# One core, conv attention and tanh attention: the planner of a hand-ordered kernel gets new spans, a longer hand-over between engines, and another rank for the score products

## The reference, cut to what matters

```python
# layer 0: conv attention (per image, HW = 4096)
e1, e2, asm = prelu(w1 @ gn(x)), prelu(w2 @ gn(x)), prelu(wa @ gn(x))
x = x + softmax(e1^T e2, axis=2) @ asm
# layer 1: additive (tanh) attention over earlier tokens
t = tokens(x);  n = layernorm(t)
f, g = n @ W1[:128], n @ W1[128:]              # 16 units each
scores[i, j] = sum_a w2[a] * tanh(f[i, a] + g[j, a] + b1[a]) + b2
t = t + (exp(scores) * (j < i)) @ n / sum_j(...)
# layer 1: 64 experts, each takes its 8 strongest tokens, two dense layers with gelu
```

## Time and profile before

| | |
|---|---|
| median of 3 runs | 5871.09 us (5862.58 to 5873.55) |
| the profiled execution, its own time | 5872.08 us |
| its span | 5869.9 us |
| PE busy | 5078.5 us |
| ACT busy | 4930.1 us |
| DVE busy | 2663.9 us |
| POOL busy | 2001.5 us |
| mean granted TensorE clock | 0.96 |

### The profile page before, as it was taken

How to read it: one execution, slowest core, us unless ns; L and a number is a source line. 1 busy time by engine, 2 the same in 40 slices (tenths; PEclk the granted TensorE clock), 3 DMA queues, 4 the chain that set the end, 5 groups by cost and what they waited for, 6 DMA issues and landing times. The chain is left out here.

```text
span 5869.9 us, 71555 instructions
## 1 busy us (share of the span) xinstructions
PE 5078.5 (87%) x28567; PEld 1726.0 (29%) x28567; DVE 2663.9 (45%) x3558; ACT 4930.1 (84%) x4186; POOL 2001.5 (34%) x1643
## 2 busy tenths in 40 slices
PE   6999988889999978899999987889999987666657
PEld 2333332223333323222333333222333332111113
DVE  8853474433454466443453466443354454000132
ACT  0139969999989969999959969999978969999970
POOL 1474431125454431113464441112555451111110
PEclk8999999999999999999999999999999999888977
DMA  0000000000000010000000010000000010000028
GB/s 29 12 18 8 8 29 1 1 8 6 13 19 10 9 40 8 1 1 8 19 19 4 12 44 8 1 1 8 10 22 10 12 38 17 1 1 1 6 101 283
DMA packets 39418, 123.99 MB, mean 21 GB/s; under 512 B 4464, under 2 KB 5424, under 8 KB 31984
## 3 DMA queue, kind: packets, MB, share of 16 engines
q1 hardware_dynamic: 38272, 119.03, 6.1%
q10 hardware_dynamic: 816, 0.39, 0.0%
HBM read 89.85 MB, written 29.56 MB: 20 GB/s over the span
## 5 line engine op out<-in xcount | busy, mean ns | idle before, releaser
L890 ACT ACTIVATE tanh_slots<-query_part,key_part 128x2048 f32<-128x2048 f32 (+41 forms) x3072 | 4151.5, 1449 | 149.0 <-DVE key_part L1293 101.5
L946 PE MATMUL ps<-tanh_slots,packed 128*32 128x512 f32 (+2 forms) x18432 | 2080.7, 588 | 457.4 <-ACT tanh_slots L890 449.5
L846 POOL TENSOR_TENSOR context_and_exp_sums<-context_and_exp_sums,exp_scores 128x512 f32<-128x512 f32 (+3 forms) x544 | 632.8, 1185 | 2043.4 <-ACT exp_scores L902 1615.5
L946 PEld LDWEIGHTS ps<-tanh_slots,packed 128*32 128x32 f32 x18432 | 541.2, 113 | 1931.1 <-ACT tanh_slots L890 1094.3
L1369 DVE TENSOR_TENSOR _tokens_second_and_probs<-ps,e_and_minus_max 128x1024 f32<-128x1024 f32 x512 | 624.5, 1220 | 1059.5 <-PE ps L981 534.4
L859 POOL TENSOR_TENSOR conv_prob_sums<-conv_prob_sums,_tokens_second_and_probs 128x512 f32<-128x512 f32 x480 | 613.6, 1278 | 1151.6 <-ACT _tokens_second_and_probs L907 1146.5
L981 PE MATMUL ps<-_tokens_second_and_probs,asm_tokens 128*128 128x512 f32 x2048 | 995.6, 612 | 6.8 <-ACT _tokens_second_and_probs L907 6.8
L907 ACT ACTIVATE _tokens_second_and_probs<-_tokens_second_and_probs 128x1024 f32<-128x1024 f32 x512 | 549.2, 1073 | 454.2 <-DVE _tokens_second_and_probs L1369 454.1
L1345 DVE TENSOR_REDUCE row_max_parts<-ps 128x1 f32<-128x1024 f32 x512 | 608.4, 1220 | 452.6 <-PE ps L1060 440.6
L1205 DVE TENSOR_TENSOR context_and_exp_sums<-context_and_exp_sums,ps 128x512 f32<-128x512 f32 (+3 forms) x544 | 344.7, 638 | 717.6 <-PE ps L957 713.3
L861 POOL TENSOR_TENSOR conv_prob_sums<-conv_prob_sums,_tokens_second_and_probs 128x512 f32<-128x512 f32 x480 | 617.6, 1287 | 37.7
(11 more groups left out here) (156 smaller groups left out, 2062.4 us busy)
## 6 DMA issues: line engine op xcount, KB each, us to landing
y_scratch<-residual_chunks SPq DMA_DIRECT2D x64, 256.0 KB, 2.0
tanh_slots<-in_wg SPq DMA_DIRECT2D x16, 1024.0 KB, 10.5
residual_chunks<-y_scratch SPq DMA_DIRECT2D x63, 256.0 KB, 2.7
residual_chunks<-in_x SPq DMA_DIRECT2D x32, 256.0 KB, 2.8
e_and_minus_max<-p_scratch SPq DMA_DIRECT2D x32, 256.0 KB, 3.3
query_part<-in_x SPq DMA_DIRECT2D x4, 1024.0 KB, 6.0
normed_tokens_first<-in_x SPq DMA_DIRECT2D x4, 1024.0 KB, 8.5
p_scratch<-e_twice SPq DMA_DIRECT2D x4, 1024.0 KB, 6.8
```

What stands on the lines that cost most here:

```text
L846: pool.tensor_tensor(dst, dst, src, ALU.add).then_inc(s_ds, 1)
L890: nc.scalar.activation(S[:, 4 * (R % 2) + k, q:SUP], F[:, SUP * blk.s + q:SUP * blk.s + SUP], ACT.Tanh, bias=keypart(blk.b, kg, kg + 1)).t ...
L946: last = mm(PS[32 * k:32 * k + 32, t, off:CHUNK], w2k[:, g, :], S[:, 4 * (R % 2) + k, CHUNK * t + off:CHUNK * t + CHUNK], start=(g == 0), ...
```

## The change

No instruction is added, removed or altered. `HOP` goes from 0.08 to 0.5 us, twelve planned spans change by up to 0.1 us, and the rank of `QK` goes from 4 to 2.5, which is behind `TR` and ahead of `C`, `F2a`, the `L` and gate work and `M`.

```diff
-    HOP = 0.08
+    HOP = 0.5
@@ T
-                prior_t = put("ACT", "T", (R, k), 0.1 + 0.833e-3 * (SUP - x.start(k, g)), behind, 4)
+                prior_t = put("ACT", "T", (R, k), 0.19 + 0.833e-3 * (SUP - x.start(k, g)), behind, 4)
@@ TR
-                prior_tr = put("PE", "TR", (R, t), 0.03 + 0.86 * w, behind, 2)
+                prior_tr = put("PE", "TR", (R, t), 0.02 + 0.89 * w, behind, 2)
@@ E, K, C
-        prior_e = put("ACT", "E", (n, t), 0.12 + 0.45 * w, behind, 1)
+        prior_e = put("ACT", "E", (n, t), 0.19 + 0.43 * w, behind, 1)
-            done.append(put("DVE", "K", (n, t), 0.35, [prior_e], 0))
-        put("PE", "C", (n, t), 0.05 + 0.86 * w, done, 3)
+            done.append(put("DVE", "K", (n, t), 0.3, [prior_e], 0))
+        put("PE", "C", (n, t), 0.07 + 0.88 * w, done, 3)
@@ conv pairs
-                put("PE", "QK", (P,), 1.1, behind, 4)
+                put("PE", "QK", (P,), 1.1, behind, 2.5)
-                put("DVE", "SM", (P,), 1.25, behind, 1)
-                put("ACT", "EX", (P,), 1.0, [("DVE", "SM", P), ("ACT", "EX", P - 1) if P else None], 2)
+                put("DVE", "SM", (P,), 1.2, behind, 1)
+                put("ACT", "EX", (P,), 1.05, [("DVE", "SM", P), ("ACT", "EX", P - 1) if P else None], 2)
-                put("POOL", "PS", (P,), 2.6 if p else 1.3, behind, 3)
+                put("POOL", "PS", (P,), 2.7 if p else 1.3, behind, 3)
@@ row maxima
-            put("PE", "M", (b, m), 0.9, behind + [("DVE", "M", b, m - 2) if m >= 2 else None], 4)
-            put("DVE", "M", (b, m), 1.25, [("PE", "M", b, m), ("DVE", "M", b, m - 1) if m else None], 4)
+            put("PE", "M", (b, m), 1.0, behind + [("DVE", "M", b, m - 2) if m >= 2 else None], 4)
+            put("DVE", "M", (b, m), 1.18, [("PE", "M", b, m), ("DVE", "M", b, m - 1) if m else None], 4)
```

## The result

The changed kernel takes 5701.1 us in the median of 4 runs (5698.74 to 5705.34), the one before 5870.94 us: a ratio of 0.9714, with a 95% interval of 0.9697 to 0.9731. The forecast was 5736 us, 35 us too slow. Of 170 us gained it foresaw 136.

A forecast was written before the change was run, and what follows sets the result against it. TensorE's pace was taken to bound the long gaps and limit what the stretches, with ACT 97 to 98% busy, could absorb. Savings 56 + 24 + 17 + 8 + 12 + 22 - 3 = 136 us from 5872.1 gave 5736, range 5650 to 5810.

The forecast's parts named there:

- The gaps: Gaps ahead of second halves shrink to 0 to 5 us, those ahead of (2, 0) and (3, 0) to near 35.
- Short halves by TensorE's work: Halves (2, 0) and (3, 0): TensorE decides, 389.2 us become 361, saving 28 us each; batches 0 and 1 save 24 and 17.
- 323 / 0.98 + 6: Short halves: last `EX` near 336 us, from 323 us TensorE work, 2% idle, 6 us for first pairs and hand-overs.
- 336 + 25: End of short halves: the 22 us chain runs beside 23 us of short tanhs, giving 361 us.
- signs of being wrong: Short stretch: `E` waiting for `C` or tanhs for `TR` above some 20 us; ACT staying at 97%; or gaps that stay.
- rivals 2 and 3: 2: dense order stalls both engines, 5823 us, chance 0.16; 3: `QK` ahead of `C` delays blocks, 5982 us, chance 0.04.
- rival 1: Stretches: TensorE's busy time is no limit and ACT alone decides; 255 us saved, 5617 us, chance 0.14.
- Long halves: Halves (1, 1) and (2, 1): 966.0 us become 960, saving 6 us each, as moved pairs must fit where TensorE is at 95%.
- and 13 more afterwards: Long halves, gate to gate: TensorE work grows by 13 us from 867.7, for `QK`, `PV`, `TR`, `C` and an `FAa`.
- The `E` of stretch (3, 1): Stretch (3, 1): `E` placed behind two tanhs instead of one saves 22 of 25 us of waits for `TR`.
- The start and (0, 1): Start: more `QK` and `PV` ahead of the gate, 3 us lost; (0, 1) with its gap: 910.1 to 902, saving 8.
- rival 2: Short halves: fixed lists wait for each other, TensorE 6% idle, 14 us more each; 5823 us in all, chance 0.16.

The follow-up runs named there:

- the late gate: The changed kernel with a batch's gate work begun only behind the last tanh of the next batch's short stretch: 5709.1 us, ratio 0.9724.

## Why the prediction was right, and where it wasn't

The measured time lies in the stated range, and the mechanism, pairs moved out of the gaps and paid for on TensorE, is what the windows show. But the nearness of the sum owes something to luck: single halves missed by up to 16 us, some up and some down.

*The gaps.* 60 `EX` leave them, and all but two close. The gaps ahead of (2, 0) and (3, 0) came out at 44 us, not 35.

*Short halves by TensorE's work.* The sum had the last `EX` at 336 us and the first tanh at 361; they came at 324.8 and 366.4. Two terms were mis-sized, in opposite directions. The first is "323 / 0.98 + 6": TensorE was busy for 319 us and idle for 5.7, so the 6 us put on top for the first pairs and hand-overs did not come, and the work was 4 us less. The second is "336 + 25": I let the chain of 22 us run beside 23 us of short tanhs, as if these took only their own time. They took 41. A block with nothing but its own tanhs goes round from `TR` over `E`, `C` and VectorE back to the next `TR` in 10 to 13.5 us, and the pairs that had filled these rounds before were gone. Some 6 us of the 41 are VectorE's gate work, by batch 1 with the late gate. Pairs put further forward thus uncover the end: the run with the old rank has its last `EX` 10 us later in the half and the first tanh 7 us sooner. In (0, 0), where 42 tanhs were left, the end took 25.2 us, as forecast, and all of the 10 us more that it saved came ahead of the last `EX` (334.6 us, forecast 345).

*The signs.* The forecast had named signs of being wrong, and two of them came. Tanhs waited for `TR` in the short half for more than 20 us:

```profile
ACT tanh_slots L890 <- PE ps L946: 24.3, 8, 4.6
```

And ACT was at 97.4% up to the last `EX` (92.6% over the half). The first sign stood for rivals 2 and 3, the second for rival 1. Of the 24.3 us, 17.0 lie behind the last `EX`, in the short blocks, where none of the rivals had put them, and the totals of the rivals (5617, 5823 and 5982 us) are far off. So the signs were badly chosen: they show the uncovered end and two engines at their limit together.

*Long halves.* Forecast 960, measured 944.4. The idle time of 84 us was right (944.4 - 860.9 = 83.5). The term that was mis-sized is the work: 867.7 us "and 13 more afterwards" turned out as 860.9, 20 less than the sum. Some 5 or 6 of them stand in the short half: TensorE was to be busy there for 345 us and was for 350.2. More of the gate work runs there now (76 of the L998 records instead of 45, and 6 of L1089 instead of none). The other 14 are gone: (1, 1) and (2, 0) together had TensorE busy for 1225.0 us before and for 1211.1 now, with 6936 and 6943 matmul records. A part is the clock. By the clock records of the trace the lower of the two levels was granted for 48 us of these halves before, with TensorE busy for 40 of them, and for 34 us now, with 28 busy. A `TR` record that followed the one before it without a pause took 0.17 us of busy time at the lower level and 0.10 at the higher, so the clock explains some 5 of the 14 us, an estimate. The rest is another sequence of the same instructions; what in it counts stays open.

I had set aside the sentence of the Trainium skill, "Perfetto Trace Analysis", "Identifying the Most-Contended Engine", by which pipelined matmuls make their busy time a bad measure. The trace sides with it on the sum of busy time. As a test of which engine is waited for, busy time did better here than the sentence would have it: in the dense part TensorE was at 99.5%, its weight loads at 35% (92.14 of 261.2 us), and with less of its work that part did become shorter, by 10 us, with ACT then at 96%.

*The `E` of stretch (3, 1).* Forecast 22, measured 24.5, and 20.5 when moved alone. The waits of tanhs and of `E` in it:

```profile
ACT tanh_slots L890 <- PE ps L946: 12.7, 8, 3.9
ACT exp_scores L902 <- PE ps L946: 3.2, 6, 1.0
```

*The start and (0, 1).* Forecast -3 and 8, measured -2.3 and 2.7. Where the 5 us of (0, 1) went I didn't look. An `EX` was put at 1.0 us, where the row has 1.07; for 4 `EX` that is nothing.

*What the forecast never asked* is which part of the change does it. The spans do: alone they give 3.35%, more than the whole. The rank gives nothing alone or next to HOP 0.5, and a few tenths of a percent with the spans and HOP 0.08. HOP 0.5 gives 1.5% alone and costs 0.9 points on top of spans and rank (0.9623 against 0.9714). It helps in (3, 1), where it puts the exponents one tanh later, and hurts in the long halves. `M` goes from TensorE to VectorE, and TensorE begins step m only when VectorE is through with step m - 2. A turn is thus the time from one step's start on TensorE to that of the next but one (the first row holds two steps):

```profile
2229.93 1.99 PE L1060 MATMUL ps<-e_and_minus_max,e_twice 64*128 64x512 f32 x8
2232.39 2.26 PE L1060 MATMUL ps<-e_and_minus_max,e_twice 64*128 64x512 f32 x8 [0.47 <-DVE row_max_parts L1345]
```

The turn takes 2.46 us. The planner has it at 1.0 + 1.18 and two hand-overs, 3.18 us with HOP 0.5 and 2.34 with 0.08. So with HOP 0.5 it spreads the 128 steps over 180 `TR`, with 0.08 over 160 to 164, and puts all pairs behind them later in ACT's list. (The kernel before had them over 184, with the old spans and HOP 0.08.) With the short hand-over for `M` alone, the long halves give 25 and 34 us more, which shows it.

## What to carry to other kernels

When a planner sets a fixed order, spans that are measured do more than a margin: ten corrected ones, the long tanh's by 5% among them (which of them counts wasn't tried), left 18 of 84 exponents in the gaps. A longer hand-over is a margin in every loop between two engines, also in those whose pace decides how soon later work begins; give it only to the edges that need it, and compare each loop's planned turn with a measured one. And what is moved out of a gap into dense work must be followed to the end of the stretch: the pairs taken forward were the filling of the short blocks' round trips.

## What I had not expected of the hardware

The same 28567 matmul records are busy for 5078.5 us in one order and 5040.5 us in another. The mean granted clocks look alike, 0.960 and 0.961, but over spans of 5870 and 5701 us they mean 475 and 446 us at the lower level, with TensorE busy for 355 and 329 of them; by the ratio of 0.17 to 0.10 us that explains some 11 of the 38 us, an estimate. It isn't only that instructions stand closer, either: the new rank alone left the span at 5864.1 us and brought the busy time to 5055.6. So a sum of TensorE busy times carries over to another order only to within 1% or so. And in stretch (2, 0) of the change TensorE and ACT were busy for 98.3% and 97.4% of 325 us at once, with both fixed lists waiting on each other. The coupling cost TensorE 1.7%, at the lower end of the 1 to 6% that forecast and rival 2 had allowed for.
